# A fused attention and FP4 feed-forward block: both row-maximum products of a half slot moved directly behind its two score products

## The reference

```
mod = (silu(c) @ wmod).reshape(32, 6, 1, 256)           # sa, ca, ga, sb, cb, gb
h = layernorm(x) * (1 + ca) + sa
q, k, v = h @ Wq + bq, h @ Wk + bk, h @ Wv + bv         # 16 heads of 16
scores = (q / 4) @ k.T + rel_bias[bucket(mem - ctx)] * 8
attn = softmax(scores)                                  # over 512 keys
x = x + ga * ((attn @ v) @ Wo + bo)
h = layernorm(x) * (1 + cb) + sb
gate, up = fp4_linear(h, w_gate), fp4_linear(h, w_up)   # 704 wide
x = x + gb * fp4_linear(silu(gate) * up, w_down)
```

## Time and profile before

| | |
|---|---|
| median of 3 runs | 3291.3 us |
| the profiled execution | 3290.7 us, of it 3288.8 us span |
| TensorE (PE) busy | 3150.3 us, 96% |
| VectorE (DVE) busy | 2822.5 us, 86% |
| ScalarE (ACT) busy | 2137.1 us, 65% |
| GpSimd (POOL) busy | 1720.8 us, 52% |
| granted TensorE clock, mean | 0.982 of full |
| L647, maxima products | 2048 of 386 ns, 789.4 us |
| L1072, the reductions | 2048 of 696 ns, 1415.9 us, and their reads, 289.4 us |

### The profile page before, as it was taken

The page is one execution under the profiler, slowest core; times in us unless marked ns, Lnnn a source line. Parts: engine busy times, 40 slices in busy tenths (PEclk is TensorE's granted clock), DMA queues, the critical chain, the costliest instruction groups (busy, mean ns, idle before and its releaser), DMA issues.

```text
span 3288.8 us, 67878 instructions
## 1 busy us (share of the span) xinstructions
PE 3150.3 (96%) x22404; PEld 1877.6 (57%) x22404; DVE 2822.5 (86%) x9960; ACT 2137.1 (65%) x3389; POOL 1720.8 (52%) x2104
## 2 busy tenths in 40 slices
PE   4899999999999999999999999999999999999985
PEld 1345565656656565655566555565665556656555
DVE  6678888888988888888888998888889888888865
ACT  2566676666666766666666666766666666666652
POOL 3415555555555555555555555555555555555455
PEclk7899999999999999999999999999999999999997
DMA  8344433334443324444233444332344423244000
GB/s 206 65 78 81 83 77 57 63 69 83 84 85 66 60 59 78 86 83 83 55 64 64 83 86 83 72 60 61 71 84 83 86 59 63 63 79 80 21 23 13
DMA packets 200187, 238.39 MB, mean 72 GB/s; under 512 B 23600, under 2 KB 178640, under 8 KB 199808
## 3 DMA queue, kind: packets, MB, share of 16 engines
q1 hardware_dynamic: 199840, 234.06, 36.9%
HBM read 164.57 MB, written 67.31 MB: 71 GB/s over the span
## 4 chain that ended last, share of the span: by engine, by line
PE 73%; issue 8%; DVE 7%; ACT 7%; POOL 4%; DMA 1%; DVEq 0%; SPq 0%; ACTq 0%; POOLq 0%
PE ps_x L676 21%; PE ps_o L665 11%; PE rings L630 11%; PE rings L647 11%; PE ps_x L704 6%; PE rings L633 4%; ACT probs L819 3%; PE ps_x L711 3%; POOL hidden L1356 2%; PE ps_x L722 1%; DVE scale L1107 1%; ACT tanh L928 1%; ACT magic L847 1%; DVE row_max L1072 1%; DVE hidden L1177 1%
## 5 line engine op out<-in xcount | busy, mean ns | idle before, releaser
L1072 DVE CUSTOM_DVE_ANT_0 rings<-rings,band_z 128x512 f32<-128x512 f32 x2048 | 1415.9, 696 | 98.2 <-issue 95.2
L819 ACT ACTIVATE probs<-rings 128x1024 f32<-128x1024 f32 x1024 | 1048.0, 1023 | 435.9 <-PE rings L633 434.8
L647 PE MATMUL rings<-k_rows,q_rows 120*128 120x512 bf16 x2048 | 789.4, 386 | 26.3 <-DVE row_max L1072 24.4
L630 PE MATMUL rings<-q_rows,k_rows 121*128 121x512 bf16 x2048 | 702.7, 383 | 30.5 <-ACT probs L819 28.0
L633 PEld LDWEIGHTS rings<-rev,band_t 128*128 128x128 f16 x5632 | 409.6, 98 | 289.4 <-issue 0.8
L665 PE MATMUL ps_o<-probs,values 128*32 128x512 f32 x4096 | 545.6, 605 | 0.0
L633 PE MATMUL rings<-rev,band_t 128*128 128x64 f16 x5632 | 500.7, 192 | 0.0
L647 PEld LDWEIGHTS rings<-k_rows,q_rows 120*128 120x128 bf16 x2048 | 197.2, 96 | 493.6 <-DVE row_max L1072 380.7
L1356 POOL TENSOR_TENSOR hidden<-hidden,inv 128x704 f32<-128x704 f32 x128 | 178.4, 1394 | 446.2 <-DVE inv L1111 446.2
L676 PE MATMUL ps_x<-w_gu_h,xq_h 128*128 128x512 f32 (+1 forms) x768 | 356.8, 465 | 1.1 <-DVE xq_l L1117 1.1
L1171 DVE SCALAR_TENSOR_TENSOR tanh<-tanh,ps_x 128x256 f32<-128x256 f32 (+1 forms) x384 | 152.7, 398 | 165.4 <-ACT tanh L928 163.2
(11 more groups left out here) (180 smaller groups left out, 6557.2 us busy)
## 6 DMA issues: line engine op xcount, KB each, us to landing
parts_dram<-parts SPq DMA_DIRECT2D x128, 384.0 KB, 2.6
q_rows<-parts_dram SPq DMA_DIRECT2D x384, 128.0 KB, 5.5
k_rows<-parts_dram SPq DMA_DIRECT2D x384, 128.0 KB, 8.0
mod_rows<-mod_rows_dram SPq DMA_DIRECT2D x32, 640.0 KB, 10.1
x_in<-in_x SPq DMA_DIRECT2D x32, 512.0 KB, 5.3
x_mid<-in_x SPq DMA_DIRECT2D x128, 128.0 KB, 2.0
out<-x_mid SPq DMA_DIRECT2D x128, 128.0 KB, 2.5
k_rows<-band_dram SPq DMA_DIRECT2D x2, 1024.0 KB, 9.5
```

Of the source, the lines that this page charges most:

```text
L630: mm(ps_s[:, bank, :], kr[0:ROW_MAX + 1, h, k0:k0 + P], qr[0:ROW_MAX + 1, h, :], start=True, stop=False)
L647: mm(ps_m[:, bank, :], q_rows[par][0:ROW_MAX, h, j * P:(j + 1) * P], k_rows[par][0:ROW_MAX, h, :], start=True, stop=True).then_inc(mscores ...
L819: A(prob_pair(s, j), ps_s, ACT.Exp).then_inc(exp_done, 1)
L1072: v.tensor_tensor_reduce(ps, ps, band_z[:, bias:bias + S], 1.0, LOWEST, ALU.add, ALU.max, row_max[:, par, 4 * h + j:4 * h + j + 1]).then_i ...
```

## The change

In TensorE's `emit`, the call for the maxima product of each position becomes two calls at the even positions and none at the odd ones:

```
--- before.py
+++ after.py
@@ -765,7 +765,9 @@
                         if j % 2 == 0 and it.has(0):
                             scores(it, s, j)
                             scores(it, s, j + 1)
-                        maxima(it, s, j)
+                        if j % 2 == 0:
+                            maxima(it, s, j)
+                            maxima(it, s, j + 1)
                         for slot, pos, kind in JOBS:
                             if (slot, pos) == (s, j):
                                 job(it, s, kind)
```

## The result

The changed kernel takes 3495.0 us in the median of four runs (3493.4 to 3496.5), against 3291.1 us for the kernel before, measured beside it: 1.0621 times the time, with a 95% interval of 1.0606 to 1.0635. That is 204 us slower. The forecast was 3488 us in a range of 3415 to 3560. The profiled execution took 3496.45 us, with a span of 3494.6 us.

A forecast was written before the change was run, and what follows sets the result against it. TensorE's queue was taken to bound the kernel, so a wait put into it is paid in full. Terms summed to 6.47 us per iteration, times 30.5 gives 197 us, hence 3488 us (range 3415 to 3560).

The forecast's parts named there:

- slots 3, 7, 11, first half: Second maxima product waits 1.15 us in each for a reduction behind VectorE's low part; 3.45 us per iteration.
- slot 15, both halves: Second maxima products wait for late reductions: 1.07 us in the first half, 0.79 us more in the second.
- slots 1, 9, 13, second half: Later job g0 delays tanh, gate product and reduction by 0.23 us; second product waits 0.39 us each, 1.17 per iteration.
- slot 0's wait for the exponential: Slot 0's scores already waited for a late exponential; slot 15's delay hides this, giving back 0.37 us per iteration.
- six neighbourhoods: Four xqT transposes and two xT jobs directly follow the product with the values, 0.06 us each, 0.36 per iteration.
- upper bound: Up to nine other second products with little slack could each wait some 0.25 us, 2.3 us per iteration.
- iteration 0 at half: First of 31 iterations counted half, since TensorE is less busy and waits hide one another; 30.5 x 6.47 = 197 us.
- falling clock: Rival, 3%: TensorE's clock falls to 0.90, 10.8 us more per iteration, 3820 us.
- the releases move up: Rival, 4%: VectorE starts reductions earlier, banks come free in time, exponentials come sooner; faster, 3274 us.
- only neighbours: Rival, 4%: stalls are hidden, only 0.36 less 0.37 us per iteration remains; no change, 3291 us.
- half absorbed: Rival, 7%: only part of the waits in slots 3, 7, 11, 15 lands; 1 to 4 us per iteration, 3320 to 3413 us.
- more stalls: Rival, 6%: late even jobs delay further reductions, over 8.8 us per iteration, above 3560 us.

The follow-up runs named there:

- the run with the neighbour alone: Kernel before, with transposes xqT put in front of the position 1 maxima product in slots 0, 4, 8, 12 and no pairs: 3296.4 us, 1.0019.
- kernel with second halves alone: Against the kernel before, maxima products paired only in the second half of each slot, first halves unchanged: 3456.0 us, 1.0499.
- the halves: Two kernels against the kernel before, maxima products paired only in first halves of slots (3441.0 us) or only in second halves (3456.0 us).
- kernel with one reduction moved up: Changed kernel, with the last reduction of slots 2, 6, 10, 14 put in front of VectorE's low part: 3399.0 us, 1.0331.

## Why the prediction was right

Its mechanism was shown from both sides: with TensorE's order kept and the reductions moved, the time falls from 3495 back to 3307; with VectorE's order kept and the even job put between the first halves' products again, from 3441 to 3322. Its terms, in means over the middle iterations (waits from start to start less 0.22 us):

| term, us per iteration | forecast | measured |
|---|---|---|
| slots 3, 7, 11, first half | 3.45 | 1.21 + 1.20 + 1.24 = 3.65 |
| slot 15, both halves | 1.07 + 0.79 | 1.32 + 0.95 |
| slots 1, 9, 13, second half | 1.17 | 3 x 0.36 = 1.09 |
| slots 2, 10, 14, second half | not named | 0.06 + 0.07 + 0.18 = 0.31 |
| slot 0's wait for the exponential | -0.37 | -0.37 |
| waits for exponentials ahead of slots 3, 11, 15 | not named | -0.32 |
| small waits in slot 15, both halves | not named | -0.24 |
| six neighbourhoods | +0.36 | +0.31 |
| one iteration | +6.47 | +6.6 |

*Slots 3, 7, 11 and slot 15* came a little larger, by 0.05 to 0.09 us each in the first three and by 0.25 and 0.16 in slot 15. Most of it is the same time under another name: in slots 3 and 11 the wait for the exponential just ahead became shorter by 0.07 us each. In slot 15's first half that wait became shorter by 0.18 us, and a wait of 0.09 in front of its first product went too, 0.27 together; in its second half two waits of 0.11 and 0.04 went. Where a queue waits less ahead of a product whose bank comes free at the same time as ever, it waits more at that product. This is read from the two traces and was not tried by itself. The 0.09 and the 0.04 are waits for reductions, which the prediction said TensorE never has before the change: the release at 1547.03 and 1547.08 in its own text is the first of them, and the record hides it, since what stands ahead of it on TensorE is recorded longer than its step.

*Slots 1, 9, 13* and the free *slot 5* were as forecast. *Three further half slots*, 2, 10 and 14, wait 0.31 us together. The prediction held them in its upper bound of nine such products at 0.25, and they took a seventh of it. *Slots 0, 4, 8 and 12* it did not price at all. They pay nothing in the changed kernel, but only because the waits just ahead of them cover theirs: paired without the others, slot 0 alone costs 0.86 us. That the sum came out in spite of this is in part luck.

*Slot 0's give-back* and the *neighbour* were right. For the neighbour the profile shows 0.16 us from the first transpose to the second, where it had 0.11, and the run with the neighbour alone gives 0.045 us in each place that nothing covers, against the 0.06 of the earlier trace rows.

The measured rows sum to 6.7 us. The 0.1 over 6.6 lies in differences at many steps and was not followed. Over the program, from the start of one block of 64 maxima products to the next, the change adds -0.8 us in the first (iteration -1), 4.8 and 5.3 in the next two, 6.6 in each of 28, and 10.6 from the start of the last block to the end. So *iteration 0 at half* was too low by 1.6 us and the next one at full too high by 1.2. The last block, which the sum held at 6.5, pays 4 us more, which was not followed, and the terms' sizes make 28 x 0.13 = 4 us. With the -0.8 that is some 7 us, the distance between 3488 and 3495. Two small slips of the text itself: its low end is 3418 by its own terms and not 3415, and 12.8 us per 2400 are 16 us over 31 iterations and not 17. Neither changes anything.

*VectorE's busy time* was expected unchanged and is 1.8 us lower in the iteration (84.61 against 86.40), with the same 309 instructions. It had taken durations to stay when nothing is added; the one that moved most is told below.

*The clock* was expected at 1.00, with no term for it in the sum, and ahead of the runs only the earlier trace rows spoke for that. The changed kernel's is 1.00 from 600 to 3000 us, with eight pauses per iteration of 0.36 to 1.32 us in the mean. The margin was narrower than the 3% for a falling clock suggests: slot 15's second wait is 1.88 us when it stands alone, and in that kernel the granted clock fell to 0.98 over 400 us; only the wait in slot 15's first half shortens it to 0.95. The kernel with second halves alone is the nearest to the rival of a falling clock, and there too the price was 1.5 us per iteration and not the 10.8 of that rival.

*The rivals* fall by the waits at L647: "the releases move up" and "only neighbours" would have left none, "half absorbed" would have left under 4 us per iteration, and "more stalls" would have shown over 8.8 us per iteration.

## What to carry to other kernels

Where two engines hand a pool of buffers to and fro, a product that is moved up in the queue of the busiest engine is worth what its release allows: lay the old end of the releasing instruction beside the new place of the one that waits, slot by slot, and the difference is the price (here 1.15 us in slots 3, 7 and 11, against 1.20 to 1.24 measured). Then follow the delay along the queue: a wait covers those that come right behind it, and prices of single places do not add up (150 and 165 us for the halves, 204 for both). Work between two users of the same ring is cover and not delay (119 of 150 us came back with the even job between them). If the order of one engine has to change, change that of the engine which frees the buffers with it (188 of 204 us came back), and for each moved job look up whose buffer the jobs near it now take over (v1 waited 0.49 us for such a bank).

## What the runs showed of the hardware

- In the kernel with second halves alone, a pause of 1.88 us in slot 15, ahead of the down products, was followed by steps of 0.21 us instead of 0.12 per product for about 3.4 us, at a granted clock of 0.50 (1522.2 to 1525.0 us); the iteration shown at 0.98 took 1.49 us more than its neighbour at 1.00. Between 600 and 3000 us the clock fell like this behind 20 of its 24 pauses of that length, to 0.50 to 0.61 over the 3.3 us from 0.5 us behind each. The changed kernel's pauses of 1.31 to 1.33 us in slot 15, three of 1.52 to 1.56 in slots 7 and 11 (ahead of 684.91, 1382.89 and 2340.43 us), and those of 1.55 in slot 15 of the kernel with one reduction moved up left the clock at 1.00 (the last from 600 to 3000 us, columns as above):

```profile
600.00:3000.00 2400.00, 2331.55 (x16708) 1389.68 (x16706) 2012.38 (x7396) 1592.38 (x2517) 1258.07 (x1557) 1.00 0.38 70
```

  What apart from the length of the pause decides it is open: in four iterations of the kernel with second halves, at 2544.79, 2645.60, 2848.63 and 2949.34 us, the clock stayed at 1.00 after the same pause.
- The 204 us of the whole change are less than the 150 and 165 us of its halves together. Slot 15's second wait of 1.88 us shrinks to 0.95 once its first product is late, and in slots 3, 7 and 11 the first half's wait covers the second half's.
- One and the same VectorE instruction got faster without being touched, the addition to x_mid at L1142. Its group in the kernel before, and in the changed one (count, busy time, mean ns, idle before):

```profile
L1142 DVE TENSOR_TENSOR x_mid<-tanh,x_mid 128x256 f32<-128x256 f32 x128 | 133.4, 1042 | 13.3
```

```profile
L1144 DVE TENSOR_TENSOR x_mid<-tanh,x_mid 128x256 f32<-128x256 f32 x128 | 63.2, 494 | 13.3
```

1042 ns against 494, four times per iteration: 2.2 us, enough for the whole fall of VectorE's busy time by 1.8. Its length follows what runs beside it on GpSimd. In slot 13, before and after:

```profile
1535.51 1.17 POOL L1286 TENSOR_TENSOR proj<-proj,parts 128x512 f32<-128x512 f32 x1
1535.61 1.35 DVE L1142 TENSOR_TENSOR x_mid<-tanh,x_mid 128x256 f32<-128x256 f32 x1
```

```profile
1629.13 0.43 DVE L1144 TENSOR_TENSOR x_mid<-tanh,x_mid 128x256 f32<-128x256 f32 x1
1629.23 1.36 POOL L1288 TENSOR_TENSOR proj<-proj,parts 128x512 f32<-128x512 f32 x1 [0.47 <-ACT parts L893]
```

Where a GpSimd instruction is running when the addition starts (126 of 128 in the kernel before, 35 in the changed one), the addition ends 0.27 to 0.29 us behind that instruction's end, every time. Where none is running (2 and 93), it takes 0.42 or 0.43 us. In slot 13 of the changed kernel it starts first, and the GpSimd instruction takes 1.36 us instead of 1.17. This is read from the traces; no run moved the two apart.
- A maxima product that waits starts 0.05 to 0.07 us after the end of the reduction that frees its bank, in all 186 waits at L647 of the changed kernel from 600 to 3000 us, and 0.06 in 165 of them (as 1563.58 to 1563.64).
- The first of the float32 transposes xqT and xT behind the product with the values (32 output columns) takes 0.16 us to the next one, in place of the 0.11 behind a maxima product: two xqT take 0.44 us against 0.38, the four of xT0 0.65 (at 1578.62 us in the changed kernel) against 0.60.
